# A second table cleared in halves, a fifth raw weight slot and a third for the remaining rows, with a smaller descriptor scratch

## The chip, the cores and the metric

The kernel runs on one core of one Trainium2 chip. The time is device microseconds of that core from the start of the program to its end. The matrix engine is called PE here, the vector engine DVE, the scalar engine ACT, GpSimd is POOL and the sync engine, which does nothing but start transfers, is SP. DRAM means the chip's HBM. All arrays are float32; on PE a product is made of three passes over pairs of a high and a low part (`_hi`, `_lo`).

## The reference

Four batches of 512 tokens with 512 features go through cross attention, and then through a mixture of 64 experts with 6 experts a token, and a shared expert.

```
x = x + attention(layernorm(x), keys and values: the context (512 rows) and the new rows (512))
def moe(x):                                    # T = 2048 tokens, E = 64, K = 6, CAP = 128, I = 192
    topk_w, topk_idx = top_k(softmax(x @ gate_w.T), 6)
    buf_tok, buf_w = slots of each expert: up to 128 (token, weight), in token order
    gx = x[buf_tok]                            # (64, 128, 512)
    g, u = split(gx @ gate_up_proj)            # 512 -> 2 * 192 per expert
    eo = (silu(g) * u) @ down_proj * buf_w     # 192 -> 512
    routed = zeros.at[buf_tok].add(eo)
    shared = (silu(x @ shared_gate.T) * (x @ shared_up.T)) @ shared_down.T
    return routed + shared
x = x + moe(layernorm(x))
```

## The kernel before

The program has two parts that share the engines' queues.

**Attention and router** (`attention_and_router`). A loop over the four batches (`body(b, more)` exists once for each engine). In each batch PE computes scores, the new values, transposed probabilities, the attended values (`av`), the output projection (`wo`), and already the next batch's q, k and v. Weights and context come through a staging buffer with two slots (`load_item`, line 352), which ACT and DVE split into high and low parts. Two rearrangements are done by small transfers: `move_pair` (line 324, sixteen transfers of 64 KB, eight from SP and eight from ACT) brings blocks of the first two probability tiles from `res` into `pT_lo`, and `move_xnT` (line 334) does the like for the next batch's normalized rows. After the `wo` products SP stores the base rows into the output and the normalized rows into the DRAM array `x2_rows` (lines 381 and 383), then keeps the transposed rows (`x2T_kept`, line 388) and loads `wv'` for the next batch. POOL scatters the routing records into a DRAM table (line 480).

**Experts** (`experts`). For each of the 64 experts POOL gathers its 128 rows from `x2_rows` (line 1434), PE transposes them and makes the gate and up products (`ps_gu`), ACT and DVE make the hidden values, PE the down product (`ps_dn`), and ACT scales it into one of six output buffers (`eo`, line 1530). POOL then adds these rows to DRAM by an indirect transfer with an add (`add_rows`, lines 1441 and 1442). The adds go in turn into two tables, the output and `second_sum`, and an add into a table waits until the one before into the same table has landed (`added[r % 2]`). 76 adds are made so, those of the 64 experts and of 12 tiles of the shared expert. When they are all done, `second_sum` is merged into the output.

POOL's queue is in order: the gather of expert e+9 stands ahead of the add of expert e. ACT writes output buffer r only after add r-6 has landed.

**The weights.** `load_weights(sp, n)` (lines 1366 to 1373) starts the load of expert n into slot n % 4 of `raw` (128 rows of 2048 values, 1.05 MB) once the slot's old content is split (`weights_split`, piece `dn` of expert n-4). For every second expert it also loads `rest` (0.26 MB), the last 64 rows of the down weights of two experts, into one of two slots. ACT writes the high part of each piece (line 1490 for gate and up, 1493 and 1495 for down), DVE the low part (line 1574). Slots 0 to 2 lie in memory that is free before the last batch ends; slot 3 lies where the router works, so the loads of experts 3 and on wait for `routed`.

**The second table** must hold zeros before the first add. SP fills it at the start of the program, from the zero rows behind `x2_rows`, with one transfer of 2048 rows and one of 128 rows (lines 411 and 413), behind the pad rows it waits for (`pads_stored`) and ahead of the first batch's transfers.

Of the kernel before, what the change touches and what calls it, by code (L numbers as in the profile page):

```python
# [29 lines left out]
P = 128  # L30
# [72 lines left out]
def attention_and_router(nc, ctx, sem, t, table, x2_rows, second_sum, x2T_kept, kept):  # L103
# [223 lines left out]
    def move_xnT(queue, b, first, past):  # L327
# [3 lines left out]
        for a in range(first, past):  # L331
            for q in range(QUADS):
                here = blocks[a * SQ:(a + 1) * SQ, :, :, :].rearrange("p (c q) t j -> p q c (t j)", q=QUADS)
                queue.dma_start(plain(tokens_of(a)[1][q * SQ:(q + 1) * SQ, :, :]),
                                here[:, q, :, :]).then_inc(xnT_moved[a], 16)

    def sync(sp, before_last_rows):
        def load_item(b, key, name, source_batch=None):
# [15 lines left out]
        def body(b, more):  # L354
# [15 lines left out]
            if more:  # L370
                load_item(b, more, "ctxT'", b + 1)
                move_xnT(sp, b, 0, 2)
                for name in ("wq'", "wk'"):
                    load_item(b, more, name, b + 1)
            if not more:
                for name in ("sg", "su", "sd"):
                    load_item(b, more, name)
                before_last_rows(sp)
# [21 lines left out]
        for name in FIRST_ITEMS[1:]:  # L400
# [7 lines left out]
        sp.dma_start(t["out"][T:ROWS, :], zero_rows).then_inc(pads_stored, 16)  # L408
        sp.wait_ge(pads_stored, 48)
        zeros = x2_rows[T:ROWS, :]  # L410
        sp.dma_start(second_sum[0:T, :].rearrange("(n p) d -> n p d", p=P),
                     zeros.unsqueeze(0).to_broadcast([T // P, P, D])).then_inc(kept.sum_cleared, 16)
        sp.dma_start(second_sum[T:ROWS, :], zeros).then_inc(kept.sum_cleared, 16)
        for b in range(B - 1):
# [781 lines left out]
ROW = GU + D  # L1196
RAW = 4
GU_SLOTS = 2
# [68 lines left out]
def experts(nc, ctx, sem, t, table, x2_rows, second_sum, x2T_kept, kept):  # L1267
# [9 lines left out]
    raw = [sb(f"raw{n}", [P, ROW]) for n in range(2)]  # L1277
    rest = [sb(f"rest{n}", [P, D]) for n in range(2)]
    gu = [(halves(sb("gu_hi0", [P, GU], F32R)), halves(sb("gu_lo0", [P, GU], F32R)))]
# [5 lines left out]
    for to, name in ((ssilu, "ssilu"), (shid, "shid")):  # L1285
        for n in range(2):
            sb(f"above_{name}{n}", [P, 3 * D])
            to.append(sb(f"{name}{n}", [P, D])[:, :])
    raw.append(sb("raw3", [P, ROW]))
    eo_above = sb("eo_above", [P, D])  # L1290
# [26 lines left out]

    raw_loaded = [sem(f"raw_loaded{n}") for n in range(RAW)]
    rest_loaded = [sem(f"rest_loaded{n}") for n in range(2)]
    gathered = [sem(f"gathered{n}") for n in range(XG)]  # L1320
# [45 lines left out]
    def load_weights(sp, n):  # L1366
        if n >= RAW:
            sp.wait_ge(weights_split, PIECE_NO["dn", n - RAW, 0] + 1)
        sp.dma_start(raw[n % RAW][:, :], t["expert"][n], max_dma_last_dim=4096).then_inc(raw_loaded[n % RAW], 16)
        if n % 2 == 0:  # L1370
            if n >= 4:
                sp.wait_ge(weights_split, PIECE_NO["dn", n - 3, 0] + 1)
            sp.dma_start(rest[n // 2 % 2][:, :], t["rest"][n // 2]).then_inc(rest_loaded[n // 2 % 2], 16)

# [18 lines left out]
    def sync(sp):  # L1393

        sp.wait_ge(kept.group_full, kept.projected)
        load_weights(sp, 2)

        sp.wait_ge(sup_full, 3)
        load_x2T(sp, 1)

        sp.wait_ge(kept.routed, 1)
        for n in range(3, 7):
            load_weights(sp, n)
        for e in range(E):
            if e + 7 < E:
                load_weights(sp, e + 7)
        sp.wait_ge(sup_full, 6)
        load_x2T(sp, 2)

        out_of_last = t["out"][LAST * S:(LAST + 1) * S, :].rearrange("(i p) d -> p i d", p=P)  # L1410
        sp.wait_ge(weights_split, len(PIECES))
        sp.wait_ge(chains_done, 1)
        sp.dma_start(base_rows, out_of_last).then_inc(out_loaded, 16)
        for n, tile in enumerate(TILES_OF[LAST]):
            r = SET_NO["shared", tile]
            sp.wait_ge(tile_added, n + 1)
            sp.dma_start(out_of_last[:, tile[1], :], eo[r % EO]).then_inc(tiles_stored, 16)
# [5 lines left out]
    def gpsimd(pool):  # L1423
# [29 lines left out]
        for e in range(3):  # L1453
            gather(e)
        pool.wait_ge(kept.sum_cleared, 32)
        gather(3)
# [29 lines left out]
    def act_weights(act, first, past):  # L1486
        for kind, n, part in PIECES[first:past]:
            act.wait_ge(raw_loaded[n % RAW], n // RAW * 16 + 16)
            if kind == "gu":
                act.activation(gu[n % GU_SLOTS][0][part], gate_up_of(n, part), ACT.Copy).then_inc(weights_high, 1)  # L1490
            else:
                hi, (own_rows, _) = dn[n % DN_SLOTS][0], rest_rows(n)
                act.activation(hi[:, 0:D], raw[n % RAW][:, GU:ROW], ACT.Copy)  # L1493
                act.wait_ge(rest_loaded[n // 2 % 2], n // 4 * 16 + 16)
                act.activation(hi[own_rows, D:2 * D], rest[n // 2 % 2][own_rows, :], ACT.Copy).then_inc(weights_high, 1)  # L1495

# [79 lines left out]
    def dve_weights(dve, first, past):  # L1576
        for kind, n, part in PIECES[first:past]:
# [4 lines left out]
            else:  # L1582
                (hi, lo), (own_rows, other_rows) = dn[n % DN_SLOTS], rest_rows(n)
                subtract(dve, lo[:, :], raw[n % RAW][:, GU:ROW], hi[:, 0:D])
                subtract(dve, hi[other_rows, D:2 * D], rest[n // 2 % 2][own_rows, :],
                         hi[own_rows, D:2 * D]).then_inc(weights_split, 1)
# [216 lines left out]
def build(nc, t):  # L1803
# [4 lines left out]
    with ExitStack() as ctx:  # L1808
# [8 lines left out]
        kept.tab = ctx.enter_context(nc.sbuf_tensor("tab", [P, E, 2], F32))  # L1817
        kept.idx_all = ctx.enter_context(nc.sbuf_tensor("idx_all", [P, E + T // P], I32))
        kept.tab_loaded = sem("tab_loaded")

# [73 lines left out]
```

## Time and profile before

| | |
|---|---|
| median of 3 runs | 797.64 us (796.4 to 797.65) |
| the profiled execution's own time | 801.92 us |
| its span, first to last instruction | 800.2 us |
| mean granted PE clock | 0.984 |
| PE busy | 758.1 us (95%) |
| DVE busy | 604.1 us (75%) |
| ACT busy | 449.7 us (56%) |
| POOL busy | 318.5 us (40%) |
| transfers | 188.75 MB, mean 236 GB/s |

The median is of runs without the profiler. All other numbers come from the profiled execution, whose own time is 4.3 us above the median. PE is busy for nearly the whole span, so the places that matter are those where it isn't, and those at the end where other work sets the time. The transfers' share is low in the attention part and over 0.9 from 440 us to 750 us. In the second section of a page the span is cut in 40 slices of 20 us, so slice 4 is 60 to 80 us. An engine's idle time is named in brackets behind the instruction that ended it, with what that instruction had waited for.

### The profile page before, as it was taken

How to read it: one execution, taken by the hardware profiler on the slowest of the kernel's cores; microseconds unless marked ns; L12 is line 12 of the kernel's file. 1: busy time of each engine (PE TensorE's matmuls, PEld its weight loads, DVE VectorE, ACT ScalarE, POOL GpSimd, SP SyncE). 2: the span in 40 equal slices, each digit the busy share in tenths (PEclk: the TensorE clock that was granted, in tenths of full speed). 3: DMA queues.
4: the chain of work that ended last, by engine and by line, in shares of the span. 5: the costliest groups of instructions: out<-in, count | busy, mean ns of one | idle time of the engine just before them, and what ended most of it. 6: DMA issues, size and time to landing. Idle time of an engine off the chain costs nothing.

```text
span 800.2 us, 10843 instructions
## 1 busy us (share of the span) xinstructions
PE 758.1 (95%) x3774; PEld 640.8 (80%) x3774; DVE 604.1 (75%) x1191; ACT 449.7 (56%) x795; POOL 318.5 (40%) x256
## 2 busy tenths in 40 slices
PE   6998999999999999999999999999999999998972
PEld 5886877878888787888788789998888898887752
DVE  6545575895768866785577899999999999998622
ACT  3425323253332433344153899999899898988610
POOL 1000010348104351055315556556666577555530
PEclk9999999999999999999999999999999999999997
DMA  4895435545436356343466999999999999999888
GB/s 164 292 239 142 126 138 210 131 133 159 190 126 159 107 170 242 113 95 130 169 231 179 318 349 349 350 357 354 344 356 344 350 347 355 343 352 339 212 178 190
DMA packets 84757, 188.75 MB, mean 236 GB/s; under 512 B 26000, under 2 KB 32528, under 8 KB 81040
## 3 DMA queue, kind: packets, MB, share of 16 engines
q1 hardware_dynamic: 53488, 143.41, 49.8%
q0 software_dynamic: 19056, 40.98, 22.1%
q10 hardware_dynamic: 12160, 3.67, 2.3%
q8 instruction: 31, 0.51, 0.3%
q14 instruction: 22, 0.18, 0.1%
HBM read 144.38 MB, written 43.92 MB: 235 GB/s over the span
## 4 chain that ended last, share of the span: by engine, by line
PE 59%; DMA 12%; DVE 7%; issue 6%; POOL 6%; ACT 5%; ACTq 2%; SPq 0%; POOLq 0%; DVEq 0%
PE bank L1189 9%; PE bank L1191 9%; PE bank L1190 9%; DMA raw<-expert_in 7%; PE ps_gu L1189 3%; PE scores L1189 3%; PE ps_gu L1191 3%; PE ps_gu L1190 3%; PE scores L1191 3%; PE scores L1190 3%; POOL second_sum L1442 2%; POOL out_rows L1442 2%; PE bank L1005 2%; DVE gu_lo L1574 2%; PE bank L1168 1%
## 5 line engine op out<-in xcount | busy, mean ns | idle before, releaser
L480 POOL DMA_INDIRECT table<-rows,slot x72 | 84.7, 1177 | 145.0 <-DVEq L929 112.7
L1574 DVE TENSOR_TENSOR gu_lo<-raw,gu_hi 128x768 fp32r<-128x768 f32 x126 | 120.1, 955 | 14.2 <-ACT gu_hi L1490 13.2
L1490 ACT ACTIVATE gu_hi<-raw 128x768 fp32r<-128x768 f32 x128 | 107.3, 841 | 7.4 <-DMA raw<-expert_in 7.3
L1189 PE MATMUL ps_gu<-gu_hi,xgT_hi 128*128 128x384 f32 x256 | 91.8, 358 | 0.0
L1191 PE MATMUL ps_gu<-gu_hi,xgT_lo 128*128 128x384 f32 x256 | 86.8, 339 | 0.0
L1190 PE MATMUL ps_gu<-gu_lo,xgT_hi 128*128 128x384 f32 x256 | 86.5, 338 | 0.0
L508 ACT ACTIVATE qT<-bank 128x512 fp32r<-128x512 f32 x32 | 19.1, 597 | 109.1 <-PE bank L1191 78.1
L1434 POOL DMA_INDIRECT xg<-x_rows,idx_all x39 | 46.7, 1198 | 42.2 <-DVEq L750 17.4
L1442 POOL DMA_INDIRECT out_rows<-product,idx_all x25 | 44.4, 1774 | 36.5 <-DMA out_rows<-product,idx_all 17.3
L513 ACT ACTIVATE pbuf<-scores,negmax 128x1024 f32<-128x1024 f32 x16 | 17.8, 1113 | 65.2 <-DVE negmax L679 48.4
L651 DVE TENSOR_TENSOR qT<-bank,qT 128x512 fp32r<-128x512 f32 x32 | 22.0, 688 | 41.2 <-ACT qT L508 41.2
L1190 PEld LDWEIGHTS ps_gu<-gu_lo,xgT_hi 128*128 128x128 f32 x256 | 48.6, 190 | 0.0
L1189 PEld LDWEIGHTS ps_gu<-gu_hi,xgT_hi 128*128 128x128 f32 x256 | 48.4, 189 | 0.0
L1191 PEld LDWEIGHTS ps_gu<-gu_hi,xgT_lo 128*128 128x128 f32 x256 | 48.4, 189 | 0.0
L1574 DVE TENSOR_TENSOR dn_lo<-raw,dn_hi 128x512 fp32r<-128x512 f32 x64 | 43.9, 687 | 2.5 <-ACT dn_hi L1495 1.9
L1574 DVE TENSOR_TENSOR dn_hi<-rest,dn_hi 64x512 fp32r<-64x512 f32 x64 | 43.9, 687 | 0.9
L1189 PE MATMUL bank<-xnT_hi,w_hi 128*128 128x512 f32 x112 | 44.2, 395 | 0.0
L1574 DVE TENSOR_TENSOR xgT_lo<-ps_xgT,xgT_hi 128x512 fp32r<-128x512 f32 x64 | 43.8, 684 | 0.2 <-ACT xgT_hi L1509 0.2
L1191 PE MATMUL bank<-xnT_hi,w_lo 128*128 128x512 f32 x112 | 43.7, 390 | 0.0
L1190 PE MATMUL bank<-xnT_lo,w_hi 128*128 128x512 f32 x112 | 43.6, 389 | 0.0
L1493 ACT ACTIVATE dn_hi<-raw 128x512 fp32r<-128x512 f32 x64 | 40.5, 633 | 2.7 <-DVEq L774 2.7
L644 DVE TENSOR_TENSOR w_lo<-stage,w_hi 128x2048 fp32r<-128x2048 f32 x16 | 36.5, 2289 | 7.1 <-ACT w_hi L500 7.0
(293 smaller groups left out, 2214.3 us busy)
## 6 DMA issues: line engine op xcount, KB each, us to landing
raw<-expert_in SPq DMA_DIRECT2D x64, 1024.0 KB, 13.4
rest<-rest_in SPq DMA_DIRECT2D x32, 256.0 KB, 9.9
x_rows<-pbuf SPq DMA_DIRECT2D x17, 256.0 KB, 2.1
xn<-x_in SPq DMA_DIRECT2D x16, 256.0 KB, 5.0
stage<-wkT_in SPq DMA_DIRECT2D x4, 1024.0 KB, 4.9
stage<-ctxT_in SPq DMA_DIRECT2D x4, 1024.0 KB, 7.4
stage<-wvT_in SPq DMA_DIRECT2D x4, 1024.0 KB, 9.0
stage<-ctx_in SPq DMA_DIRECT2D x4, 1024.0 KB, 10.3
```

The costliest lines, as they stand in the source:

```text
L480: pool.indirect_dma_start(out=table, out_offset=bass.IndirectOffsetOnAxis(ap=slot[:, i, k:k + 1], axis=0), in_=rows[:, i, k, :], in_offset ...
L508: act.activation(split_dest(group)[0], split_source(key, group), ACT.Copy).then_inc(high_done, 1)
L644: dve.tensor_tensor(lo, item_stage(key, name), hi.bitcast(F32), ALU.subtract).then_inc(item_low, 1)
L651: dve.tensor_tensor(lo, split_source(key, group), hi.bitcast(F32), ALU.subtract).then_inc(group_taken, 1)
L1189: pe.matmul(out, still[0], moving[0], start=first, stop=False)
L1190: pe.matmul(out, still[0], moving[1], start=False, stop=False)
L1191: return pe.matmul(out, still[1], moving[0], start=False, stop=last)
L1434: pool.indirect_dma_start(out=xg[e % XG], out_offset=None, in_=x2_rows, in_offset=index(("expert", e))).then_inc(gathered[e % XG], 16)
L1442: pool.indirect_dma_start(out=(t["out"], second_sum)[r % 2], out_offset=index(what), in_=eo[r % EO], in_offset=None, compute_op=ALU.add).t ...
L1490: act.activation(gu[n % GU_SLOTS][0][part], gate_up_of(n, part), ACT.Copy).then_inc(weights_high, 1)
L1493: act.activation(hi[:, 0:D], raw[n % RAW][:, GU:ROW], ACT.Copy)
L1574: return dve.tensor_tensor(lo, x, hi.bitcast(F32), ALU.subtract)
```

## The change

- The clearing of `second_sum` leaves the start. A new function `clear_sum(sp, b)` is called in the bodies of the second and third batch (b = 1 and 2), behind the load of `wk'`. Each call clears 1024 rows; the first also clears the 128 rows behind them.
- The scratch for the descriptors of POOL's transfers is set to 4096 bytes a partition; before it was left at its default, which is larger.
- The memory goes to `raw` slot 3 and a third `rest` slot, which now lie outside both parts' working memory. A slot 4 of `raw` takes the place where slot 3 was.
- The load of expert 3 no longer waits for `routed` and stands right behind that of expert 2. Load n waits for the split of expert n-5, `rest` n for that of n-5 too (before n-4 and n-3).
- POOL waits for `sum_cleared` at 48, since there are three transfers now.

```diff
+    def clear_sum(sp, b):
+        zeros = x2_rows[T:ROWS, :]
+        if b == 1:
+            sp.wait_ge(pads_stored, 48)
+            sp.dma_start(second_sum[T:ROWS, :], zeros).then_inc(kept.sum_cleared, 16)
+        half = T // P // 2
+        sp.dma_start(second_sum[(b - 1) * half * P:b * half * P, :].rearrange("(n p) d -> n p d", p=P),
+                     zeros.unsqueeze(0).to_broadcast([half, P, D])).then_inc(kept.sum_cleared, 16)
...
                 for name in ("wq'", "wk'"):
                     load_item(b, more, name, b + 1)
+                if b:
+                    clear_sum(sp, b)
...
-        sp.wait_ge(pads_stored, 48)
-        zeros = x2_rows[T:ROWS, :]
-        sp.dma_start(second_sum[0:T, :].rearrange("(n p) d -> n p d", p=P),
-                     zeros.unsqueeze(0).to_broadcast([T // P, P, D])).then_inc(kept.sum_cleared, 16)
-        sp.dma_start(second_sum[T:ROWS, :], zeros).then_inc(kept.sum_cleared, 16)
...
-RAW = 4
+RAW = 5
+REST = 3
...
-            if n >= 4:
-                sp.wait_ge(weights_split, PIECE_NO["dn", n - 3, 0] + 1)
-            sp.dma_start(rest[n // 2 % 2][:, :], t["rest"][n // 2]).then_inc(rest_loaded[n // 2 % 2], 16)
+            if n >= 2 * REST:
+                sp.wait_ge(weights_split, PIECE_NO["dn", n - 2 * REST + 1, 0] + 1)
+            sp.dma_start(rest[n // 2 % REST][:, :], t["rest"][n // 2]).then_inc(rest_loaded[n // 2 % REST], 16)
...
         load_weights(sp, 2)
+        load_weights(sp, 3)
...
         sp.wait_ge(kept.routed, 1)
-        for n in range(3, 7):
+        for n in range(4, E):
             load_weights(sp, n)
-        for e in range(E):
-            if e + 7 < E:
-                load_weights(sp, e + 7)
...
-        pool.wait_ge(kept.sum_cleared, 32)
+        pool.wait_ge(kept.sum_cleared, 48)
...
+        kept.raw3 = ctx.enter_context(nc.sbuf_tensor("raw3", [P, ROW], F32))
+        kept.rest2 = ctx.enter_context(nc.sbuf_tensor("rest2", [P, D], F32))
...
-    nc = bacc.Bacc("TRN2", target_bir_lowering=False, num_devices=1)
+    nc = bacc.Bacc("TRN2", target_bir_lowering=False, num_devices=1, dynamic_dma_scratch_size=4096)
```

PE, DVE, ACT and POOL keep the order of their instructions. Only SP's changes, at three places. Line numbers differ by 9 to 12 between the two programs.

The first place is SP's queue at the start of the program, in the first batch, before. `x_rows` is `x2_rows`, `pbuf` holds the pads, `ctx_in` is the context and `xn<-x_in` the second batch's rows:

```order
L406 DMA table<-pbuf 128x128 [waits const_ready]
L407 DMA x_rows<-pbuf 128x512
L408 DMA out_rows<-pbuf 128x512
L411 DMA second_sum<-x_rows 16x4x16384 [waits pads_stored]
L413 DMA second_sum<-x_rows 16x4096
L352 DMA stage<-ctx_in 128x4x512 [waits item_low]
L364 DMA xn<-x_in 32x4x512 [waits group_taken]
```

and the same place now:

```order
L418 DMA table<-pbuf 128x128 [waits const_ready]
L419 DMA x_rows<-pbuf 128x512
L420 DMA out_rows<-pbuf 128x512
L362 DMA stage<-ctx_in 128x4x512 [waits item_low]
L374 DMA xn<-x_in 32x4x512 [waits group_taken]
```

The two clearing transfers and the wait for the pads are gone from here; the context load follows the pads at once.

The second place is SP's queue in the second batch, between the last weight load and the stores of base rows and normalized rows. Before, the stores followed that load:

```order
L352 DMA stage<-wkT_in 128x2048 [waits item_low]
L381 DMA out_rows<-res 128x512 [waits base_ready]
L383 DMA x_rows<-pbuf 128x512 [waits x2_ready]
L381 DMA out_rows<-res 128x512 [waits base_ready]
L383 DMA x_rows<-pbuf 128x512 [waits x2_ready]
```

Now:

```order
L362 DMA stage<-wkT_in 128x2048 [waits item_low]
L342 DMA second_sum<-x_rows 16x4096 [waits pads_stored]
L344 DMA second_sum<-x_rows 8x4x16384
L393 DMA out_rows<-res 128x512 [waits base_ready]
L395 DMA x_rows<-pbuf 128x512 [waits x2_ready]
```

The clearing of one half stands there. Its outermost dimension is 8, where that of the single transfer was 16. The third batch has the like, without the small transfer.

The third place is SP's queue where the experts begin, from the load of expert 2 on (`raw2`, `rest1` are slots; `v_hi` and `v_lo` take kept transposed rows). Before:

```order
L1369 DMA raw2<-expert_in 128x2x1024 [waits group_full]
L1373 DMA rest1<-rest_in 128x512
L1379 DMA v_hi<-x2T_kept 128x2x1024 [waits sup_full]
L1379 DMA v_lo<-x2T_kept 128x2x1024
L1369 DMA raw3<-expert_in 128x2x1024 [waits routed]
L1369 DMA raw0<-expert_in 128x2x1024 [waits weights_split]
L1373 DMA rest0<-rest_in 128x512 [waits weights_split]
```

Now:

```order
L1378 DMA raw2<-expert_in 128x2x1024 [waits group_full]
L1382 DMA rest1<-rest_in 128x512
L1378 DMA raw3<-expert_in 128x2x1024
L1388 DMA v_hi<-x2T_kept 128x2x1024 [waits sup_full]
L1388 DMA v_lo<-x2T_kept 128x2x1024
L1378 DMA raw4<-expert_in 128x2x1024 [waits routed]
L1382 DMA rest2<-rest_in 128x512
L1378 DMA raw0<-expert_in 128x2x1024 [waits weights_split]
```

Expert 3's load has moved ahead of the two transposed rows' loads, and expert 4's load and its `rest` are the first behind `routed`, without a wait for a split.

## Rows read from the trace of the kernel before

**Rows 1.** Busy time by stage: window, its length, engines, granted clock, transfers' share, GB/s.

```profile
480.00:560.00 80.00, 79.82 (x445) 71.73 (x444) 77.95 (x138) 73.81 (x138) 48.52 (x35) 1.00 1.06 353
560.00:740.00 180.00, 173.68 (x948) 153.00 (x946) 166.59 (x295) 162.37 (x302) 111.36 (x74) 0.99 1.06 348
```

**Rows 2.** PE in order of time: start, duration, instruction, idle before and releaser.

```profile
71.40 1.58 PE L1005 MATMUL bank<-ident,pbuf 128*128 128x128 f32 x8 [3.57 <-DVE v_lo L651]
264.88 1.16 PE L1005 MATMUL bank<-ident,pbuf 128*128 128x128 f32 x8 [0.33 <-DVE v_lo L651]
```

**Rows 3.** Chain that ended last, first and third batch: start, duration, what.

```profile
52.10 1.21 ACT pbuf L513 x2
...
60.58 6.16 DMA pT_lo<-res
...
248.82 1.20 ACT pbuf L513 x2
...
256.58 3.65 DMA pT_lo<-res
```

**Rows 4.** The 2048 rows' clearing transfer: its issue, and its landing.

```profile
L411 SPq DMA_DIRECT2D second_sum<-x_rows x1: 651/651/651, 31.6 to 31.6; - x1
...
DMA to landing us min/median/max: 15.7/15.7/15.7
```

**Rows 5.** SP's issues in order of time: start, duration, transfer.

```profile
104.51 0.34 SPq L381 DMA_DIRECT2D out_rows<-res  x1
...
192.83 0.33 SPq L352 DMA_DIRECT2D stage<-wkT_in  x1
...
216.10 0.93 SPq L352 DMA_DIRECT2D stage<-wvT_in  x1
...
296.98 0.34 SPq L381 DMA_DIRECT2D out_rows<-res  x1
...
735.37 0.47 SPq L1379 DMA_DIRECT2D pT_lo<-x2T_kept  x1
```

**Rows 6.** Windows as in Rows 1: after PE's pause, and the same work in batch three.

```profile
72.00:76.00 4.00, 4.00 (x14) 3.34 (x14) 3.97 (x7) 1.19 (x2) 0.00 (x0) 0.57 0.47 197
268.00:272.00 4.00, 3.88 (x18) 2.92 (x17) 3.88 (x11) 2.40 (x2) 1.05 (x1) 1.00 0.00 0
```

**Rows 7.** POOL's adds in order of time, columns as in Rows 2.

```profile
541.84 1.58 POOL L1442 DMA_INDIRECT out_rows<-product,idx_all  x1 [0.30 <-issue]
...
753.50 1.55 POOL L1442 DMA_INDIRECT out_rows<-product,idx_all  x1 [2.11 <-DMA out_rows<-eo,idx_all]
...
765.96 1.55 POOL L1442 DMA_INDIRECT second_sum<-eo,idx_all  x1 [0.79 <-DMA second_sum<-product,idx_all]
```

**Rows 8.** Landing of line 1442's adds issued in 472:496, 541.8:753.4 and 753.4:768.

```profile
DMA to landing us min/median/max: 8.2/8.6/9.1
...
DMA to landing us min/median/max: 5.5/8.5/10.0
...
DMA to landing us min/median/max: 4.7/4.9/5.1
```

**Rows 9.** Landing of raw weight loads (line 1369) issued in 440:480 and 700:740.

```profile
DMA to landing us min/median/max: 7.3/12.0/12.8
...
DMA to landing us min/median/max: 11.1/14.1/15.0
```

**Rows 10.** Landing of the last two kept rows' loads, issued at 734.7 and 735.4.

```profile
DMA to landing us min/median/max: 13.1/15.4/17.7
```

**Rows 11.** ACT's waits in 560:740: us in total, times, longest.

```profile
ACT gu_hi L1490 <- DMA raw<-expert_in: 7.3, 12, 1.3
...
ACT product L1530 <- DMA second_sum<-product,idx_all: 2.3, 1, 2.3
```

**Rows 12.** Windows as in Rows 1: before the routing is ready, and right behind it.

```profile
402.00:420.00 18.00, 18.00 (x113) 15.43 (x111) 14.57 (x39) 11.06 (x27) 3.62 (x2) 1.00 0.58 217
440.00:445.00 5.00, 3.39 (x25) 3.10 (x24) 3.03 (x6) 3.31 (x6) 3.32 (x3) 1.00 0.84 250
```

More of the change, by code:

```diff
@@ L1277, in experts @@
     raw = [sb(f"raw{n}", [P, ROW]) for n in range(2)]
-    rest = [sb(f"rest{n}", [P, D]) for n in range(2)]
+    rest = [sb(f"rest{n}", [P, D]) for n in range(2)] + [kept.rest2]
     gu = [(halves(sb("gu_hi0", [P, GU], F32R)), halves(sb("gu_lo0", [P, GU], F32R)))]
@@ L1288, in experts @@
             to.append(sb(f"{name}{n}", [P, D])[:, :])
-    raw.append(sb("raw3", [P, ROW]))
+    raw.append(kept.raw3)
+    raw.append(sb("raw4", [P, ROW]))
     eo_above = sb("eo_above", [P, D])
@@ L1318, in experts @@
     raw_loaded = [sem(f"raw_loaded{n}") for n in range(RAW)]
-    rest_loaded = [sem(f"rest_loaded{n}") for n in range(2)]
+    rest_loaded = [sem(f"rest_loaded{n}") for n in range(REST)]
     gathered = [sem(f"gathered{n}") for n in range(XG)]
@@ L1493, in act_weights @@
                 act.activation(hi[:, 0:D], raw[n % RAW][:, GU:ROW], ACT.Copy)
-                act.wait_ge(rest_loaded[n // 2 % 2], n // 4 * 16 + 16)
-                act.activation(hi[own_rows, D:2 * D], rest[n // 2 % 2][own_rows, :], ACT.Copy).then_inc(weights_high, 1)
+                act.wait_ge(rest_loaded[n // 2 % REST], n // 2 // REST * 16 + 16)
+                act.activation(hi[own_rows, D:2 * D], rest[n // 2 % REST][own_rows, :], ACT.Copy).then_inc(weights_high, 1)
     def act_silu(act, n):
@@ L1584, in dve_weights @@
                 subtract(dve, lo[:, :], raw[n % RAW][:, GU:ROW], hi[:, 0:D])
-                subtract(dve, hi[other_rows, D:2 * D], rest[n // 2 % 2][own_rows, :],
+                subtract(dve, hi[other_rows, D:2 * D], rest[n // 2 % REST][own_rows, :],
                          hi[own_rows, D:2 * D]).then_inc(weights_split, 1)
```

## The prediction

> **What bounds the kernel now.** I read first the busy time by stage. From 480 to 560 us PE works 79.82 of 80 us; from 560 to 740 us it works 173.68 of 180, so 6.3 us are idle, and the transfers' share stands at 1.06 in both [rows 1]. The stage is held by two things that nearly agree. Then I read PE in order of time for its pauses in the attention part. There is one that the other batches lack: 3.57 us before 71.40, against 0.33 us at the same instruction of the third batch [rows 2]. The chain that ended last says why: the last `move_pair` transfer takes 6.16 us to land in the first batch and 3.65 us in the third [rows 3]. Ahead of it on SP's queue stands the clearing transfer, issued at 31.6 us and landed 15.7 us later, with 3 MB of context, rows and `wo` weights behind it [rows 4].
>
> Last I read POOL's adds. From 541.84 to 753.50 us 48 adds are issued, 4.41 us each [rows 7], and each lands 8.5 us (median) after its issue [rows 8]. Two tables take turns, so a landing of 8.5 us with a little for the release gives one add in 4.4 us: in this stretch POOL issues as fast as landings allow. When the last weight and kept rows have landed (735.37 + 17.7 = 753.1 us [rows 5, 10]), adds land in 4.9 us [rows 8], and the last five come in 12.46 us, 2.49 us each [rows 7]. The merging of the tables begins behind the last add at 765.96, so the end of the kernel is set by when the adds are done, not by when PE is.
>
> **The change, part by part.**
>
> *Clearing leaves the start.* The way from the second exponential to the first store of base rows is 104.51 - 52.10 = 52.41 us in the first batch and 296.98 - 248.82 = 48.16 us in the third, the same instructions both times [rows 3, 5]. The difference, 4.25 us, is the price of the queue in front of the pair moves and what it drags along: 3.57 - 0.33 = 3.24 us of PE's pause [rows 2], and the rest from the granted clock, which is 0.57 in the four us behind the pause and 1.00 in the third batch [rows 6]. With 15.7 us of transfer gone, context and `wo` are in before the moves, which start behind the exponential at 52.10. I take 4.25 us. The lower end is the landing alone, 6.16 - 3.65 = 2.5 us. The upper end is the pause and the slow clock's whole loss, 3.24 + 0.43 * 4 = 5.0 us; DVE, busy 3.97 of 4 us there, hides part of the latter [rows 6]. PE is the bound until the experts, so all of it arrives.
>
> *The halves come back in batches two and three.* Two transfers and one small one are issued behind the load of `wk'` (192.83 us in the second batch). Behind them on the queue are stores nobody reads before the next batch's second half, and at 216.10 the load of `wv'`, for which 23 us pass [rows 5]. At the rate of the single transfer a half takes 15.7 / 2 = 7.9 us [rows 4]. Even a half that took the full 15.7 us would be in by 209. I take 0, hidden by PE's own products; what it costs without that cover is a rival below.
>
> *Expert 3's load moves ahead of the routing.* It is 1.05 MB and falls into 402 to 420 us, where the transfers' share is 0.58 [rows 12], so it fits there. It leaves the stretch from 441 to 753 us, where every MB costs 1 / 348 GB/s = 2.87 us [rows 1]: 3.0 us. Expert 4's `rest` (0.26 MB) now starts at the routing instead of at the split of expert 1, into the five us with 250 GB/s [rows 12]: up to 0.75 us. The last load is then in 3.7 us earlier, at 749.4 us by the clock of before. But the adds of that stretch are paced by their landings. In 3.7 us at 4.41 there are 0.84 adds fewer done; from there each takes 2.49. The gain at the end is 3.7 * (1 - 2.49 / 4.41) = 1.6 us. Bounds: 0, if the loads land no earlier; 3.7, if the adds follow in full.
>
> *A fifth `raw` and a third `rest` slot.* They give each load one expert more of time. ACT waited 7.3 us in twelve pieces for raw weights in 560:740 [rows 11], and PE's 6.3 idle us are mostly these passed on. They go, and what is late next are the adds: ACT also waited 2.3 us for an add to free its output buffer [rows 11], and an earlier PE reaches that wait sooner. So I take 0 for the slots beyond the 1.6 us. Below nothing: more loads in the queue might slow the adds. Raw landings grew from 12.0 us (440:480) to 14.1 us (700:740) [rows 9] while adds landed in 8.6 us early (472:496) and 8.5 us later [rows 8], so the trace shows no such effect; upper end of the gain 6.3 us.
>
> The Trainium skill (DMA: Bandwidth & Descriptors, "Queues, rings and completion order") says that each engine goes round-robin over the queue rows it has work for, packet by packet. By that rule a deeper SP queue costs the adds nothing, while by one shared line they would grow with the raw landings; the rows of the two landings agree with the rule, and it lowers the chance I give the slower rival.
>
> *A smaller descriptor scratch.* The trace does not show it. If POOL never waits for room it costs 0; the nearest row is the 0.30 us issue gap ahead of an add [rows 7]: once more per add it gives 24 * 0.30 = 7.2 us over 24 turns of each table. At most two adds and a few gathers are in the air at once, so I take 0.
>
> **Sum.** 4.25 + 1.6 = 5.85 us. Against its own time the profiled execution would go from 801.92 to 796.1 us. The median of the runs is 4.3 us lower, 797.64, and goes to 791.8 us. What this kernel's measurement can tell from no change is about 0.2%, 1.6 us.
>
> **The rivals.**
>
> *The adds follow.* The adds are late only because the weights are, and PE's 6.3 us come out at the end beside the head's 4.25: 10.6 us, 787.1 us. For it: the raw waits [rows 11]. Against it: POOL's waits for landings in the same stretch.
>
> *The adds land later* (slower than before). A fifth load in the air takes turns of the engines from the adds. There are 24 turns of each table in the stretch, and each 0.1 us on a landing costs 2.4 us. The gain of 5.85 us is eaten at 0.24 us; at +0.5 us (8.5 to 9.0) it is 12 - 5.85 = 6.2 us slower, 803.8 us. A scratch that makes POOL wait (+7.2 us) would end near 799. Against it: the unchanged landings [rows 8, 9].
>
> *The clearing only moves.* The halves hold up batches two and three as the whole did the first. Each would have to reach past 216 us to make `wv'` late; then two halves cost about what the whole did, 4.25 us, and what stays is 1.6 us: 796.0 us. Against it: 23 us of room [rows 5].
>
> The Trainium skill (the same page, "Why a DMA increments its semaphore by 16 and not by 1") says that a transfer runs on the largest number of engines up to 16 that divides the slowest dimension of both patterns. The halves' outermost size is 8, so by that page they run on 8 engines and take 15.7 us where 16 engines would take 7.9. No run here shows it yet; by either the half is in before 216, which is why this rival stays small.
>
> **How the numbers follow.** Forecast 0.66, its own range 789.0 to 795.0 (2.5 to 5.0 at the head, 0 to 3.7 behind). The adds follow 0.17, later adds or scratch 0.09, the clearing only moves 0.08. The range 787.0 to 796.5 leaves out the slower case and a part of the second. Faster by over 0.2%: 0.66 + 0.17 and half of the last, some of the first's edge off, 0.85; the same 0.06; slower 0.09.
>
> **What would show it.** Head: PE's pause before the transposes of the first batch falls to about 0.3 us, the last pair move lands in under 4 us, no slow clock behind it, and the store at 104.51 comes near 100.3. Halves: no new pause of PE near 190 to 220 and 290 to 310. Prefetch: the load of expert 3 before 402 us, the last kept rows' load in 3 to 4 us earlier against the routing. Slots: ACT's wait for raw near 0, its wait for adds larger than 2.3 us, adds still 4.4 us apart, and the last add behind the routing by about 1.6 us less. It is wrong if the adds come closer than 4.2 us, if landings pass 8.7, or if the first batch keeps its pause.

## The result, and the profile after

The changed kernel takes 807.18 us (median of 4 runs, 804.78 to 808.38), the kernel before 797.64 us beside it (4 runs, 796.40 to 799.78). The ratio is 1.0105, with a 95% interval of 1.0071 to 1.0139. It is 1% slower, and the time lies 15.4 us above the prediction and 10.7 us above the top of its range. The profiled execution took 808.38 us with a span of 806.6 us, where the one before had 801.92 and 800.2. Further below, four single executions took 1256 to 1936 us (one of start_5slots, one of after_third, two of the kernel before); every ratio is of the others alone.

The lines of the attention part shown here (such as 473, 1012 and 1196 of the changed kernel) have numbers 7 above those of the kernel before; for SP's transfers it is 9 to 12.

First the stores of base rows, one per batch, since their distances give the length of each batch (SP's issues in order of time: start, duration, transfer; [rows 5] has two of those before).

```profile
101.71 0.34 SPq L393 DMA_DIRECT2D out_rows<-res  x1
...
190.68 0.73 SPq L344 DMA_DIRECT2D second_sum<-x_rows  x1
...
197.64 0.35 SPq L393 DMA_DIRECT2D out_rows<-res  x1
...
292.94 0.69 SPq L344 DMA_DIRECT2D second_sum<-x_rows  x1
...
300.59 0.34 SPq L393 DMA_DIRECT2D out_rows<-res  x1
...
402.70 0.49 SPq L393 DMA_DIRECT2D out_rows<-res  x1
```

Before, the distances were 96.46, 96.01 and 96.20 us (104.51, 200.97, 296.98, 393.18). Now they are 95.93, 102.95 and 102.11 us. The first store is 2.80 us earlier, and then 6.94 us are lost behind the first half (issued at 190.68) and 5.91 us behind the second (292.94): 12.9 us together. From the fourth store to the last add it takes 773.95 - 402.70 = 371.25 us, against 765.96 - 393.18 = 372.78 before: 1.53 us gained. From 765.96 to 773.95 at the last add that makes -2.80 - 0.53 (the batch between the first two stores) + 12.85 - 1.53 = +7.99 us. So the loss sits in the batches that the two halves stand in.

POOL in order of time, through the first of them (columns as in rows 2):

```profile
193.92 0.97 POOL L487 DMA_INDIRECT table<-rows,slot  x1 [0.30 <-issue]
206.95 1.19 POOL L473 TENSOR_TENSOR rstd<-veps,half 128x1 f32<-128x1 f32 x2 [12.06 <-DMA table<-rows,slot]
210.19 0.78 POOL L473 TENSOR_TENSOR rstd<-veps,half 128x1 f32<-128x1 f32 x1 [2.05 <-DVE veps L855]
```

The same place of the kernel before:

```profile
198.31 2.46 POOL L480 DMA_INDIRECT table<-rows,slot  x1 [0.30 <-issue]
202.22 0.57 POOL L466 TENSOR_TENSOR rstd<-veps,half 128x1 f32<-128x1 f32 x1 [1.46 <-DVE veps L848]
```

POOL's last instruction of a batch is a wait until all table scatters of that batch have landed (`scattered`), and behind it in POOL's queue stands `rstd` of the next batch's second norm. Before, the scatters landed in time and POOL waited 1.46 us, and for DVE. Now it sits idle for 12.06 us, for a scatter. The chain that ended last goes through it, and the waits from 186 to 220 us (in total, times, longest) say who waits for POOL in turn:

```profile
193.92 12.86 DMA table<-rows,slot
```

```profile
POOL rstd L473 <- DMA table<-rows,slot: 12.1, 1, 12.1
DVE pbuf L793 <- POOL rstd L473: 7.2, 2, 6.8
```

DVE stands for 6.8 us in front of the normalised rows, and PE then runs out of rows to transpose:

```profile
208.97 0.63 PE L1012 MATMUL bank<-ident,pbuf 128*128 128x128 f32 x4 [0.83 <-DVEq L851]
211.43 1.09 PE L1012 MATMUL bank<-ident,pbuf 128*128 128x128 f32 x4 [1.83 <-DVEq L851]
214.75 1.51 PE L1012 MATMUL bank<-ident,pbuf 128*128 128x128 f32 x6 [2.23 <-DVE qT L658]
...
313.26 0.63 PE L1012 MATMUL bank<-ident,pbuf 128*128 128x128 f32 x4 [1.74 <-DVEq L851]
316.59 1.69 PE L1012 MATMUL bank<-ident,pbuf 128*128 128x128 f32 x8 [2.69 <-DVE qT L658]
```

The three pauses of the second batch add up to 4.89 us, the two of the third to 4.43 us. That leaves 2.1 and 1.5 us of the 6.94 and 5.91 us, which I put down to the granted clock; no run separates them. The windows (columns as in rows 1) show the clock, and what the transfers did meanwhile:

```profile
198.00:202.00 4.00, 4.00 (x19) 3.33 (x18) 2.42 (x7) 0.00 (x0) 0.00 (x0) 1.00 0.43 180
202.00:206.00 4.00, 4.00 (x20) 3.30 (x19) 0.00 (x0) 0.55 (x1) 0.00 (x0) 1.00 0.41 161
206.00:210.00 4.00, 2.76 (x14) 1.86 (x12) 2.13 (x5) 1.02 (x3) 1.19 (x2) 1.00 0.27 102
210.00:214.00 4.00, 1.09 (x4) 0.72 (x4) 3.25 (x9) 0.82 (x2) 1.55 (x2) 0.65 0.46 177
214.00:218.00 4.00, 3.25 (x12) 2.99 (x13) 3.74 (x7) 1.87 (x3) 0.00 (x0) 0.50 0.48 185
...
314.00:318.00 4.00, 1.41 (x9) 1.26 (x9) 3.50 (x8) 1.13 (x2) 0.78 (x1) 0.87 0.67 258
318.00:322.00 4.00, 4.00 (x15) 3.22 (x14) 2.79 (x4) 2.40 (x2) 0.00 (x0) 0.70 0.41 168
```

From 198 to 206 the transfers' share is below one half at 180 and 161 GB/s: hardly anything but the half moves, on half of the engines. In the trace's packet records the half is 32 packets of 64 KB, 2.44 us each, or four on each of 8 engines. The first starts at 194.65 us and the last ends at 205.81; from the issue that is 15.1 us. The scatters' own packets take 0.01 us each, yet their last one ends only at 205.92, right behind the half. For the second half the two times are 307.64 and 307.75. POOL was released then, and the transfers' share fell to 0.27. The granted clock was 1.00 as long as PE worked. Behind the pauses it was 0.65 and 0.50 (0.50 is 1.2 GHz) in the second batch, and 0.87 and 0.70 in the third.

What the prediction had looked for at the head did happen. There is no pause of PE in front of the transposes of the first batch, against 3.57 us in [rows 2], and the window 72:76 has its full clock, against 0.57 in [rows 6]:

```profile
69.67 1.08 PE L1012 MATMUL bank<-ident,pbuf 128*128 128x128 f32 x8
```

```profile
72.00:76.00 4.00, 3.88 (x17) 2.88 (x16) 3.90 (x11) 2.24 (x2) 0.29 (x1) 1.00 0.03 10
```

In the expert part ACT waits less for raw weights, as [rows 11] had it at 7.3 us, and waits about as long for adds:

```profile
ACT gu_hi L1497 <- DMA raw<-expert_in: 3.0, 4, 1.7
ACT product L1537 <- DMA second_sum<-product,idx_all: 2.6, 1, 2.6
```

Landings of raw weights issued in 710:750, and of the adds in 551:760, in place of [rows 9] and [rows 8]:

```profile
DMA to landing us min/median/max: 14.6/17.7/18.8
```

```profile
DMA to landing us min/median/max: 4.8/8.4/9.5
```

With a fifth load in the air each load takes 3.6 us longer and an add takes no longer. From 551.4 to 758.5 us POOL issues 48 adds, 4.41 us apart as before. The last kept rows' load lands at 738.4 + 20.8 = 759.2 us, 356.5 us behind the fourth store, against 753.1 - 393.18 = 359.9 before: 3.4 us earlier, where the prediction looked for 3 to 4.

### The profile page after: what moved, and what is told of

Its sections match the earlier page's. It is cut to its first block, busy times and chain, and to the rows that moved or that the text cites. A ratio compares the mean times of both kernels' runs of the same rounds, so it can differ in the third digit from the quotient of the medians.

```text
span 806.6 us, 10844 instructions
## 1 busy us (share of the span) xinstructions
PE 762.3 (95%) x3774; PEld 642.5 (80%) x3774; DVE 603.5 (75%) x1191; ACT 449.5 (56%) x795; POOL 312.0 (39%) x256
## 4 chain that ended last, share of the span: by engine, by line
PE 54%; DMA 21%; issue 9%; POOL 7%; DVE 4%; ACT 3%; SPq 1%; POOLq 0%; DVEq 0%; ACTq 0%
PE bank L1196 9%; PE bank L1198 9%; PE bank L1197 9%; DMA second_sum<-product,idx_all 4%; DMA second_sum<-eo,idx_all 4%; PE scores L1196 3%; PE scores L1198 3%; DMA second_sum<-eo_above,idx_all 3%; PE scores L1197 3%; DMA table<-rows,slot 3%; DMA out_rows<-eo,idx_all 2%; DMA out_rows<-product,idx_all 2%; POOL out_rows L1449 2%; PE ps_gu L1196 2%; PE ps_gu L1198 2%
## 5 line engine op out<-in xcount | busy, mean ns | idle before, releaser
L1441 POOL DMA_INDIRECT xg<-x_rows,idx_all x39 | 44.9, 1152 | 41.3 <-DVEq L757 17.4
L1449 POOL DMA_INDIRECT out_rows<-product,idx_all x25 | 42.8, 1713 | 29.8 <-DMA out_rows<-product,idx_all 12.9
```

The costliest lines, as they stand in the source:

```text
L1441: pool.indirect_dma_start(out=xg[e % XG], out_offset=None, in_=x2_rows, in_offset=index(("expert", e))).then_inc(gathered[e % XG], 16)
L1449: pool.indirect_dma_start(out=(t["out"], second_sum)[r % 2], out_offset=index(what), in_=eo[r % EO], in_offset=None, compute_op=ALU.add).t ...
```

## The experiments

All ratios are to the kernel before on the same chip, in the same hour. That chip took 799.5 us for the kernel before in the last two comparisons, and 807 to 808 us in the first two, where the second, third and fourth batch had one or two further pauses of PE, mostly of 1.0 to 1.6 us, in every kernel's trace, that with the clearing at the start too. Their origin was not looked into, and the kernel before itself was not traced in those two. So each ratio is read beside its own batches. Theory: the half holds up the batch's scatters, POOL waits for them in order, and the next batch's `rstd` waits behind. Rivals: the slots or the scratch are slow; the bytes on SP's queue hold up PE's own loads; the clearing costs its batch something wherever it stands.

**Clearing at the start, slots kept** (start_5slots). The changed kernel with the clearing back where it was. In all code below `...` stands for what is left out, and the lines are against the changed kernel where nothing else is said.

```
-                if b:
-                    clear_sum(sp, b)
+        sp.dma_start(second_sum[0:T, :] ..., zeros ... [T // P, P, D])   # at the start, as before
```

> The changed kernel, with the clearing back at the start in one transfer of 2048 rows, as before; five raw slots, three rest slots and the small scratch stay. Theory A (the halves are what is slow: POOL's wait for its last table scatters, behind the halves' packets, holds up the second norm): 1.6 us less than the kernel before, 796.0 us of 797.64, POOL's wait of 12 us before its first rstd of batches two and three gone, and the last add 323 us behind the routing. Rival B (five slots or the small scratch are what is slow): it stays near 805 to 807 us.

Measured: 0.994 (0.9917 to 0.9963). POOL's wait for scatters is gone. The slots and the early load do not make the kernel slower, so the loss is the halves'. The gain is 4.9 us (3.0 to 6.7), where 1.6 was expected; the part on the slots below takes this up.

**Halves on 16 engines, packets of 64 KB** (e16_64k).

```
-        sp.dma_start(second_sum[...].rearrange("(n p) d -> n p d", p=P), zeros ... [half, P, D])
+        sp.dma_start(second_sum[...].rearrange("(n p) d -> n p d", p=64), zeros[0:64, :] ... [16, 64, D])
```

> The changed kernel, each half as 16 pieces of 64 rows (16x2x16384), so on 16 engines with two 64 KB packets each instead of 8 engines with four. Theory A: a scatter waits behind two packets instead of four; POOL's wait of 12.1 us falls to 4 to 7 us and PE's pause of 4.9 us to 0 to 2 us: 793 to 798 us. Rival C (the bytes on SP's queue are what is slow: stores behind the half): the same bytes, so PE's pause stays over 3 us and the time over 803 us.

Measured: 0.9887 (0.9858 to 0.9915).

**Halves on 8 engines, rows of 2 KB** (e8_8k).

```
+        sp.dma_start(... [8, 128, D] ..., max_dma_last_dim=2048)
```

> The changed kernel, each half still with 8 as its outermost size, but cut into rows of 2 KB (8x128x512). Theory A with the packet's length as the cause: POOL's packets get their turn between short packets; POOL's wait falls from 12.1 us to under 4 us, PE doesn't pause: 791 to 794 us. Theory A with the eight busy engines as the cause, or rival C: nothing changes, 805 to 808 us.

Measured: 0.9883 (0.9853 to 0.9913).

**Halves on 16 engines, rows of 2 KB** (e16_8k).

```
+        sp.dma_start(... [16, 64, D] ..., max_dma_last_dim=2048)
```

> The changed kernel, each half on 16 engines and in rows of 2 KB (16x64x512). Theory A: the forecast's time, 791 to 794 us, POOL's wait under 3 us. Rival B: 801 us or more. Rival C: 800 us or more.

Measured: 0.9911 (0.9879 to 0.9942). What POOL waited for in the second batch, in e16_64k, then e8_8k, then e16_8k:

```profile
POOL rstd L472 <- DMA table<-rows,slot: 7.2, 1, 7.2
```

```profile
POOL rstd L473 <- DMA table<-rows,slot: 5.5, 1, 5.5
```

```profile
POOL rstd L473 <- DMA table<-rows,slot: 5.5, 1, 5.5
```

The rivals asked for 800 us or more against 797.64, a ratio of 1.003 or more, and all three stay below 0.995. But POOL's waits are longer than was expected (4 to 7, under 4 and under 3 us). In these hours POOL waits 3.65 us there with no half at all (for DVE, in start_5slots). With either cure, 16 engines or shorter packets, less of it is left over: DVE stands for 2.2 us at most behind it in e16_64k and 0.5 to 0.6 us in the other two, and PE's pause at the transposes is 1.05 us in e16_64k and 0.2 us in the others, as in the kernel before. In the third batch POOL waits 4.3 to 4.5 us in all three. On 8 engines the packets decide, not how long the half is on its way: in e8_8k the scatters' last packet ends at 200.76 us and POOL goes on at 201.49, while the half's rows of 2 KB still come at some 100 a us until about 204. Behind 202 us twice as much moves as in `moved` (below), which has no half in that stretch. The window 202:206, first of e8_8k and then of `moved`:

```profile
202.00:206.00 4.00, 4.00 (x19) 3.30 (x19) 3.35 (x7) 0.00 (x0) 1.46 (x3) 1.00 0.70 270
```

```profile
202.00:206.00 4.00, 4.00 (x19) 3.31 (x18) 3.58 (x9) 0.00 (x0) 1.55 (x2) 1.00 0.34 131
```

What no run separates is the step inside an engine: whether a scatter's data wait for their turn behind a 64 KB packet, or only the signal that they have landed.

**The changed kernel again** (after_again), beside the next three.

> The changed kernel once more, beside three others on one chip. If what was measured is the kernel's and not the chip's: ratio to the kernel before 1.007 to 1.014, POOL again waits about 12 and 11 us for table scatters in front of the second norm's rstd of batches two and three.

Measured: 1.0016 (0.9998 to 1.0034). The expectation failed: the ratio is 0.9% lower than the first one. The waits of POOL were 9.9 and 8.3 us instead of 12.1 and 11.1. after_third below takes this up.

**POOL's wait behind the next `rstd`** (pool_order). The halves stay as they are. `free_slots(b)` holds the two lines that are taken out at the batch's end.

```
+            if b:
+                free_slots(b - 1)        # behind the next batch's rstd
-            pool.wait_ge(scattered, (b + 1) * 16 * NT * K)
-            pool.sem_inc(slots_free, 1)
+            if b == B - 2:
+                free_slots(b)
```

> The changed kernel with its halves as they are (8 engines, packets of 64 KB); only POOL's wait for the batch's scattered table rows is moved from the batch's end to behind the next batch's rstd of the second norm (the last batch keeps its place). Theory (the halves' long packets hold up the table scatters, and POOL's in-order wait for these holds up the next batch's rstd, and so DVE and PE): the scatters are as late as before, about 12 us, but nothing waits for them; the 12.9 us lost in two batches come back nearly whole, ratio 0.985 to 0.993. Rival (the long packets slow other transfers too, the copies of rows and the pair moves, and the wait at POOL is only where it is seen): half or less comes back, ratio 0.998 to 1.006, with PE's pauses of about 2 us still there behind 208 us.

Measured: 0.9896 (0.9867 to 0.9926), 9.8 us below the changed kernel beside it (798.97 against 808.79). POOL in order of time:

```profile
193.83 0.97 POOL L493 DMA_INDIRECT table<-rows,slot  x1 [0.30 <-issue]
198.47 0.57 POOL L477 TENSOR_TENSOR rstd<-veps,half 128x1 f32<-128x1 f32 x1 [3.67 <-DVE veps L861]
```

The scatters are still late: their last packet ends at 203.98 us, behind the half's at 203.68 and 5.5 us behind the start of `rstd`. The same half with the same packets passes at the same place, and costs nothing that this measurement can tell once `rstd` does not stand behind the wait. The batches take 97.72 and 97.70 us, against 103.14 and 100.02 in after_again, and PE's pause at the transposes is back at 0.2 us. The long packets by themselves slow nothing that PE needs. This is the experiment that shows the wait, not the bandwidth, to be the price.

**Halves alone** (halves_4slots). The kernel before with only the clearing moved; expert 3's load is back behind the routing too.

```
-RAW = 5
-REST = 3
+RAW = 4
-    nc = bacc.Bacc(..., dynamic_dma_scratch_size=4096)
+    nc = bacc.Bacc(...)
```

> The kernel before with only the clearing moved as in the changed kernel (halves on 8 engines, 64 KB packets, batches two and three); four raw and two rest slots, expert 3 loaded behind the routing, default scratch. Theory (halves cost 12.9 us, the freed head gives 4 to 5): 8 us slower, ratio 1.008 to 1.013, with POOL waiting about 12 us for scatters in both batches. Rival (slots or scratch have a part in the loss): ratio 1.00 to 1.005.

Measured: 1.0063 (1.0038 to 1.0089), with waits of 10.0 and 9.0 us. That is below the theory's 1.008 and above the rival's 1.005, and the waits are as short as those of after_again beside it. The slots had no part in the loss: with them the ratio is 0.47% lower (1.0063 - 1.0016).

**Halves elsewhere** (moved: 16 engines, 2 KB rows; long_moved: as in the changed kernel, 8 engines and 64 KB). Both stand behind the loads of a batch's context, in `moved` issued at 119.6 and 217.2 us, some 70 us ahead of the last scatters of their batches.

```
         load_item(b, more, "ctx", b)
+        if b in (1, 2):
+            clear_sum(sp, b)
...
-                if b:
-                    clear_sum(sp, b)
```

> The changed kernel with the halves on 16 engines in 2 KB rows, and issued right behind the loads of a batch's context, where no table scatter is under way. Theory (what counts is that no long packet stands in front of the scatters): as good as the four variants with short packets or halves out of the way, ratio 0.986 to 0.992. Rival (a half in the batch costs PE something wherever it stands, through the row copies behind it): ratio 0.995 or more.

> The changed kernel with its halves as they are (8 engines, packets of 64 KB), but issued right behind the loads of a batch's context, some 40 us ahead of the table scatters. Theory (the long packets cost nothing by themselves; they cost where the scatters of a batch are in flight with them and POOL waits for these): as the variant that has short packets at that place, ratio 0.987 to 0.994, POOL's wait in front of the second norm's rstd back at 3.7 us. Rival (a half on 8 engines costs its batch several us wherever it stands): ratio 0.998 or more.

Measured: moved 0.9915 (0.9888 to 0.9942), long_moved 0.9919 (0.9894 to 0.9943), whose batches take 95.99, 95.95 and 96.28 us. The long packets are free at a place where nobody waits for a scatter, and the rival of a price per half wherever it stands falls.

**Both cures** (both).

> The changed kernel with both cures: POOL's wait for the scatters behind the next batch's rstd, and halves on 16 engines in 2 KB rows, at the changed kernel's place. Theory (either cure takes away the whole loss): no better than either alone, ratio 0.986 to 0.992. Rival (each takes away its own part): ratio below 0.985.

Measured: 0.9904 (0.9878 to 0.993), 792.01 us. It is no better than either alone. Seven variants (this one, e16_64k, e8_8k, e16_8k, pool_order, moved, long_moved) beat both kernels with 0.988 to 0.992, and their intervals overlap.

**Scratch alone** (scratch_only). Against the kernel before.

```
-    nc = bacc.Bacc("TRN2", target_bir_lowering=False, num_devices=1)
+    nc = bacc.Bacc("TRN2", target_bir_lowering=False, num_devices=1, dynamic_dma_scratch_size=4096)
```

> The kernel before with only the descriptor scratch made 4096. Theory (POOL never waits for room in it): ratio 0.997 to 1.003, adds still 4.4 us apart. Rival (POOL waits for room, or the 0.6% that the slots' variant gained is partly the scratch's): ratio above 1.004, or below 0.997.

Measured: 0.9975 (0.9953 to 0.9997). No loss. Whether it is a gain stays open, since the kernel before itself came out at 0.9987 beside it.

**The kernel before itself** (before_again).

> The kernel before itself, to have its trace on this chip: ratio 1.000 within its interval. If the chip is slower than that of the first profile by its own pauses, the batches take 97.7 to 99.5 us from first store to first store instead of 96.0 to 96.5, with two PE pauses of about 1.5 us in each.

Measured: 0.9987 (0.9964 to 1.001), with batches of 96.10, 96.21 and 96.10 us, so the further pauses of the first two comparisons were gone. Its trace has something the first one had not. The clearing is issued at 28.61 us instead of 31.59, and the pause of 3.57 us in [rows 2] is not there:

```profile
28.61 0.65 SPq L411 DMA_DIRECT2D second_sum<-x_rows  x1
```

```profile
67.84 1.17 PE L1005 MATMUL bank<-ident,pbuf 128*128 128x128 f32 x8
```

The five traces with the clearing at the start stand in one order: issued at 31.59, 31.22, 29.46, 28.64 and 28.61 us, a pause of 3.57, 2.70, 0.66, 0.38 and none. From the second exponential to the first store they take 52.41, 51.65, 48.52, 48.22 and 47.70 us, and the twelve traces without the clearing there 47.59 to 47.76. So the head's price differs from execution to execution, from nothing to 4.8 us, and goes with the time of the issue. Nothing here shows what moves the issue, or that the issue's time alone is the cause.

**The head alone, the slots alone, and the changed kernel once more** (moved_4slots, start_5slots_2, after_third), on one chip. moved_4slots is `moved` with four raw and two rest slots and the default scratch, start_5slots_2 is start_5slots.

> The kernel before with only the clearing taken out of the start (halves on 16 engines in 2 KB rows, behind the loads of a batch's context); four raw and two rest slots. It is the head's gain by itself. Theory (what the clearing costs at the start is 0 to 4.8 us by when it is issued, 2.9 us on the mean of the traces so far): ratio 0.995 to 0.9985. Rival (the head's gain is the 4.25 us of the prediction or more in every execution): ratio 0.990 to 0.9945.

> Clearing at the start and five raw and three rest slots, a second time: the slots by themselves. Theory (the loads' lead gives 1.9 us between the fourth store of base rows and the last add, the mean of the traces so far): ratio 0.996 to 0.999. Rival (the slots give 4.8 us as in the first time): ratio 0.992 to 0.9955.

> The changed kernel a third time. Theory (the loss is POOL's wait for the scatters, and this wait is 12.1 and 11.1 us where the batches have no pauses of their own, 9.9 and 8.3 where they have): with batches of 96 us the ratio is 1.007 to 1.012 again; with batches of 98 to 99 us 1.000 to 1.004. Rival (the difference between the two measurements has nothing to do with it): the other way round.

Measured: the head alone 0.9945 (0.9922 to 0.9969), 4.4 us. My theory of 2.9 us, from the mean of the three traces with four slots, asked for 0.995 or more and is outside by a little; the value lies on the edge of the rival, and the interval holds both. The untraced runs of the kernel before give a hint: of the 24 of this comparison 19 have a mean granted clock of 0.990 or less and a median of 799.7 us, and the 5 above it 796.7 us. That would fit a pause with its slow clock in most executions and none in the others, and would explain 3.0 of the 4.4 us. It is inferred from the clock alone, and the comparison before it has only three such runs (796.6, 797.4 and 800.4 us, the others' median being 799.6). The slots alone 0.9968 (0.9944 to 0.9991), 2.6 us. The changed kernel 1.0074 (1.0048 to 1.01), with batches of 95.94, 102.90 and 101.51 us and these waits in the second and third:

```profile
POOL rstd L473 <- DMA table<-rows,slot: 12.2, 1, 12.2
```

```profile
POOL rstd L473 <- DMA table<-rows,slot: 10.6, 1, 10.6
```

So with batches of 96 us the ratio is 1.007 to 1.010, and with the longer ones of after_again, where POOL's waits are 2 to 3 us shorter, 1.002. The terms then close: 1.0074 / (0.9945 * 0.9968) = 1.0162, and 0.0162 * 799.6 = 13.0 us for the two halves, against 12.9 us from the batches in the first trace. Each of the three ratios is uncertain by 0.2 to 0.3%, the 13.0 us therefore by some 3 us; that the two agree to 0.1 us is luck.

## Why the prediction was wrong, point by point

**The head.** Forecast 4.25 us. From the second exponential (54.10 us) to the first store it takes 47.61 us in the trace after, against 52.41 before: 4.80 us. By itself it measured 4.4 us (2.5 to 6.2). The size was right, and the pause and its slow clock are gone as forecast. But it was read from one trace with the longest of the five pauses, and over the five traces the price is 2.0 us on the mean; that it fits the times so well is partly luck. The store came only 2.80 us earlier since that execution was 2.0 us later at the exponential, out of the start of the program.

**The halves.** "I take 0, hidden by PE's own products" is the step that failed, by 12.9 us. What the runs showed in its place: the table scatters land only when the half is through, POOL waits 12.06 and 11.05 us for them in order, and the next batch's `rstd`, DVE and PE stand behind (pool_order takes this wait away and with it the loss, long_moved takes the half away from it). I looked for who stands behind the halves on SP's queue, found the stores and the load of `wv'`, and both indeed came in time. What I did not ask is which other queue has transfers on the same engines in that stretch, and who waits for these. It was in the code I had before me: POOL's in-order wait for `scattered` ahead of the next `rstd`. It was in the trace too: POOL's last scatter of a batch was issued at 198.31 us, and a half issued at some 193 us with 7.9 to 15.7 us to go covers it in either case.

**The rival "the clearing only moves"** had the right place and the wrong condition. It was to begin only if a half reached past 216 us, and its price was that of the head, 4.25 us. The half was through at 206 us, and each cost some 6 us. So its chance of 0.08 stood on the wrong test, and its time of 796.0 us lay on the wrong side of no change.

**The Trainium skill's rules that I weighed.** That the halves run on 8 engines, as the Trainium skill (DMA: Bandwidth & Descriptors, "Why a DMA increments its semaphore by 16 and not by 1") has it, agrees with the trace: the share is 0.41 to 0.43 with the half alone. I used it for the length only, and there it served: 15.1 us from issue to the last packet's end beside its 15.7. The round-robin, packet by packet (the Trainium skill, the same page, "Queues, rings and completion order"), I had used to say that a deeper queue costs others nothing. For the adds that held: 8.4 us beside 8.5. But taking turns by packet says that a small transfer waits for the other queue's packet, and these were 64 KB and 2.4 us each. Both readings are in line with the rule, though neither proves it; what I left out was the packet's size.

**The early load and the slots.** Forecast 1.6 us, and 1.53 us in the first pair of traces. The mean over five traces with four slots is 371.8 us from the fourth store to the last add, over twelve with five slots 370.2 us: 1.7 us. By the times alone it was 2.6 us (0.7 to 4.5) and 4.9 us (3.0 to 6.7), 1.6 and 3 times the forecast, and the second interval leaves the forecast out. Those differences of times also hold the head's price, which differs from run to run, so the size stays open. Where a further us or more would lie is not settled; the scratch at 0.9975 is a candidate that no trace shows.

**Later adds, and the scratch.** Both rivals fell, with landings of 8.4 us and a ratio below 1.

**The sum.** With 12.9 us for the halves it would give 809.0 us for the profiled execution, which took 808.4, and 804.7 us for the median, which was 807.2. I had carried the 4.3 us between the profiled execution and the median over; in the changed kernel they were 1.2. The first trace's expensive head may be a part of those 4.3 us, but no run shows it. Without the halves' loss the forecast of 5.85 us, 0.73%, is near and rather too small: the variants without the loss measured 0.8 to 1.2%.

## What to carry to other kernels

Before a large transfer is put into a gap, list the transfers of all queues in that stretch, the small ones above all, and ask of each which engine waits for it in order, and what stands behind that wait. The gap on the issuing queue alone says nothing. Where a wait only frees a resource for later, put it behind the next urgent instruction; and cut a filler into short rows, so that small transfers pass it. Here, with rows of 2 KB, POOL's wait was 5.5 us on 8 engines as on 16.

## What was not expected of the hardware

- A copy with a repeated source of 128 rows of 2 KB went out in packets of 64 KB, 2.4 us each with one transfer on 8 engines. A scatter of another queue, 0.01 us a packet, then took 12.86 us to land, until the copy was through. With rows of 2 KB on the same 8 engines POOL's whole wait was 5.5 us.
- Pauses of PE of 0.83, 1.83 and 2.23 us within 7 us went with a granted clock of 0.65 and 0.50 in the windows 210:214 and 214:218.
- The kernel before took 807 to 808 us in two comparisons and 799.5 us in two later ones on the same chip, 1% less. The other kernels' traces of the first two have one or two more pauses of PE in three of the batches. What begins them was not looked into.
- A transfer issued at 31.6 us in one execution and at 28.6 us in another of the same kernel went with a pause of 3.57 us at 71 us in the first and none in the second. So the median of a kernel may hide two kinds of executions.
